# An attention layer followed by a graph aggregation on one core: bulk transfers moved from SP's queue to GpSimd's, and the places of eight maxima in VectorE's order changed

## What is computed

```python
q = x @ Wq.T + bq;  k = key @ Wk.T + bk;  v = value @ Wv.T + bv
s = (q @ k.T) / sqrt(4096) * adj
s = where(abs(s) < 1e-5, -1e9, s)
h = softmax(s, axis=-1) @ v @ Wm.T + bm
x1 = layernorm(x + h)
out = layernorm(x1 + relu((adj @ x1) @ W1.T + b1))
```

## Time and profile before

| | us |
|---|---|
| median of 3 executions | 2224.5 (2216.5 to 2249.4) |
| the profiled execution's own time | 2225.5 |
| its span in the trace | 2223.7 |
| TensorE matmul busy | 1986.5 (89%), 8859 matmuls |
| VectorE busy | 1545.2 (69%) |
| ScalarE busy | 872.4 (39%) |
| GpSimd busy | 107.2 (5%), 158 instructions |
| DMA queues | q1 (SP) 306.26 MB, 57.7% of the engines' span; q0 (GpSimd) 85.47 MB, 16.9% |

### The profile page before, as it was taken

One profiled execution on the slowest core, in us unless ns is written; L12 is line 12 of the kernel. 1 busy time (PEld: TensorE's weight loads), 2 busy tenths in 40 slices (PEclk: granted clock), 3 DMA queues, 4 the chain that ended last, 5 costly groups with the idle time before them and its releaser, 6 DMA issues.

```text
span 2223.7 us, 26354 instructions
## 1 busy us (share of the span) xinstructions
PE 1986.5 (89%) x8859; PEld 890.4 (40%) x8859; DVE 1545.2 (69%) x3203; ACT 872.4 (39%) x1166; POOL 107.2 (5%) x158
## 2 busy tenths in 40 slices
PE   8968998999999986989897878998897669999998
PEld 5423443444444432434333333443343224444443
DVE  7987777888888643767565656666665424888887
ACT  5765444556565433444443444444442210000000
POOL 5000000000000200000000000000000000000000
PEclk9998999999999997999999989999998889999999
DMA  8548877899999957678878798777777967555452
GB/s 304 192 143 195 227 212 197 202 260 247 260 246 257 254 129 192 126 154 159 153 145 143 144 142 154 154 164 155 141 152 153 228 168 206 119 134 144 118 124 75
DMA packets 585958, 393.21 MB, mean 177 GB/s; under 512 B 479728, under 2 KB 506352, under 8 KB 584048
## 3 DMA queue, kind: packets, MB, share of 16 engines
q1 hardware_dynamic: 565088, 306.26, 57.7%
q0 software_dynamic: 20752, 85.47, 16.9%
HBM read 190.32 MB, written 117.44 MB: 138 GB/s over the span
## 4 chain that ended last, share of the span: by engine, by line
PE 68%; DMA 10%; DVE 8%; SPq 7%; issue 5%; ACT 2%; DVEq 0%; ACTq 0%
PE ps L1042 21%; PE ps L1021 20%; PE ps L1181 15%; DMA UT<-Uhl 6%; PE ps L1053 5%; PE ps L1066 2%; PE ps L1136 2%; PE ps L974 1%; DMA PT<-Phl 1%; SPq L461 1%; SPq L457 1%; DMA x1T<-x1hl 1%; DVE prob L1937 1%; DMA kv_chunk<-in_key_t 1%; SPq L579 1%
## 5 line engine op out<-in xcount | busy, mean ns | idle before, releaser
L1042 PE MATMUL ps<-V,PT 128*128 128x512 f16 x3072 | 709.4, 381 | 7.2 <-issue 7.2
L1021 PE MATMUL ps<-KG,left 128*128 128x512 f16 x2688 | 639.8, 387 | 67.5 <-ACT ps L1378 50.9
L1042 PEld LDWEIGHTS ps<-V,PT 128*128 128x128 f16 x3072 | 301.9, 98 | 375.0 <-issue 16.7
L1021 PEld LDWEIGHTS ps<-KG,left 128*128 128x128 f16 x2688 | 266.6, 100 | 403.6 <-issue 89.9
L1385 ACT ACTIVATE small<-prob 128x512 f32<-128x512 f32 x256 | 159.1, 627 | 268.3 <-DVE prob L1937 247.7
L1965 DVE SCALAR_TENSOR_TENSOR Phl<-prob,Phl 128x2048 f16<-128x2048 f32 x64 | 146.6, 2290 | 119.6 <-ACT Phl L1398 111.9
L1053 PE MATMUL ps<-Wvm,UT 128*128 128x512 f16 x384 | 121.4, 482 | 120.9 <-issue 102.4
L1378 ACT ACTIVATE ps<-ps 128x512 f32<-128x512 f32 x192 | 111.5, 581 | 230.6 <-PE ps L1021 230.6
L1943 DVE TENSOR_SCALAR small<-small,eps_s,neg_s 128x512 f32<-128x512 f32 x256 | 137.1, 542 | 64.6 <-ACT small L1385 62.9
L2142 DVE SCALAR_TENSOR_TENSOR z_out<-ps,inv_vw,x_in 128x512 f32<-128x512 f32 x32 | 24.0, 751 | 225.8 <-PE ps L1053 225.8
L1398 ACT ACTIVATE Phl<-prob 128x2048 f16<-128x2048 f32 x64 | 121.8, 1904 | 143.7 <-DMA PT<-Phl 141.8
(11 more groups left out here) (222 smaller groups left out, 2005.6 us busy)
## 6 DMA issues: line engine op xcount, KB each, us to landing
adjh<-in_adj POOLq DMA_DIRECT2D x64, 512.0 KB, 8.1
adj_bf<-adjh SPq DMA_DIRECT2D x64, 512.0 KB, 6.0
left_dram<-left SPq DMA_DIRECT2D x16, 896.0 KB, 6.5
xraw<-in_x_t SPq DMA_DIRECT2D x8, 1024.0 KB, 8.7
t_dram<-tq POOLq DMA_DIRECT2D x8, 1024.0 KB, 5.5
t<-t_dram SPq DMA_DIRECT2D x32, 256.0 KB, 6.3
x_in<-in_x SPq DMA_DIRECT2D x32, 256.0 KB, 3.7
xb_dram<-x_in SPq DMA_DIRECT2D x32, 256.0 KB, 2.9
```

The lines of the kernel that those rows point to most:

```text
L1021: last = nc.tensor.matmul(ps[:, bank, :], left[:, s, k, d * P:(d + 1) * P], KG[gr][:, RIGHT[k], m, d, :], start=(first and n == 0), stop=( ...
L1042: last = nc.tensor.matmul(ps[:, BU + b, :], PT[:, b, s, m, :], V[:, v, m, :], start=(m == 0 and n == 0), stop=(m == MT - 1 and n == 2))
```

## The change

All plain loads and stores of both passes that stood in SP's list are issued on GpSimd's, by functions of the same names with the same waits and the same source and destination. SP keeps the transposes (and, in the aggregation, its loads of x1 rows and b1). The order of GpSimd's new list is written anew. VectorE's two maxima of a period change place, and a chunk is now loaded half a period earlier relative to its use. The load of W1 counts on another semaphore. SP's lists become:

```diff
                 for q in range(1, NP):
-                    first_period(q)
...
+                    for g in (2 * q - 2, 2 * q - 1):
+                        turn_high(g)
+                        turn_low(g)
...
                 def second_period(q):
                     i = q - NP
                     if i >= 2:
                         turn_merged_high(2 * i - 4)
                         turn_merged_low(2 * i - 4)
                     turn_high(2 * q - 2)
                     turn_low(2 * q - 2)
                     if i >= 2:
-                        load_o(2 * i - 2)
                         turn_x1_high(2 * i - 4)
-                        store_x1(2 * i - 4)
...
                         turn_x1_low(2 * i - 4)
                     turn_high(2 * q - 1)
                     turn_low(2 * q - 1)
                     if i >= 2:
                         turn_merged_high(2 * i - 3)
                         turn_merged_low(2 * i - 3)
...
                         turn_x1_high(2 * i - 3)
                         turn_x1_low(2 * i - 3)
-                    store_adj(q, 0)
-                    if q + 1 < 2 * NP:
-                        load_left(q + 1, True)
-                    store_adj(q, 1)
-                    if i >= 2:
-                        store_x1(2 * i - 3)
-                        store_y(2 * i - 4)
-                    if i >= 1:
-                        load_x_again(2 * i - 1)
```

GpSimd's new lists (in the first pass the list of SP before was `load_t`, the transposes of one block, xb, kp and left stores, adj stores, x load, the transposes of the other block, o store, xb store, chunk, x load, vp store, second loads, chunk, o store):

```diff
+                def first_period(q):
+                    load_adj(q, 0)
+                    store_left(q)
+                    if q + 1 < NP:
+                        load_t(q + 1)
+                    load_adj(q, 1)
...
+                    if q + 1 < NP:
+                        store_x_bias(2 * (q + 1))
+                    for b in range(2):
+                        store_adj(q, b)
+                    if q + 2 < NP:
+                        load_x_first(2 * (q + 2))
+                    if 2 <= q < 6:
+                        load_chunk(2 * (q - 2) + 1)
+                    if q == NP - 1:
+                        for k in range(NB):
+                            load_right(0, k)
+                    if q >= 2:
+                        store_first(2 * q - 3)
+                    if q + 1 < NP:
+                        store_x_bias(2 * (q + 1) + 1)
+                    if q + 2 < NP:
+                        load_x_first(2 * (q + 2) + 1)
+                    if FIRST_STEP <= q < FIRST_STEP + STEPS:
+                        store_second_keys(q - FIRST_STEP)
+                        store_second_values(q - FIRST_STEP)
+                    if 1 <= q < 5:
+                        load_chunk(2 * (q - 1))
+                    if q == FIRST_STEP - 1:
+                        pool.wait_ge(kv_mx, 4 * MC)
+                    if FIRST_STEP - 1 <= q < FIRST_STEP + STEPS - 1:
+                        load_second(q + 1 - FIRST_STEP)
+                    if q == NP - 1:
+                        pool.wait_ge(left_st, 16 * NP)
+                        for k in (P1, P7, P6, P2):
+                            load_right(1, k)
+                        load_left(NP, False)
+                        for k in (P5, P4):
+                            load_right(1, k)
+                        load_left(NP, True)
+                        load_right(1, P3)
+                    store_first(2 * q - 2)
...
+                def second_period(q):
+                    i = q - NP
                     for b in range(2):
                         load_adj(q, b)
...
+                    if i >= 3:
+                        store_y(2 * i - 5)
+                    if i >= 1:
+                        load_o(2 * i - 2)
                     for b in range(2):
+                        store_adj(q, b)
+                    if i >= 2:
+                        store_x1(2 * i - 4)
+                    if i >= 1:
+                        load_x_again(2 * i - 2)
+                    if i >= 3:
+                        store_sums(i - 3)
+                    if i >= 1:
+                        load_o(2 * i - 1)
+                    if q + 1 < 2 * NP:
+                        load_left(q + 1, False)
+                    if i >= 2:
+                        store_y(2 * i - 4)
+                    if i >= 1:
+                        load_x_again(2 * i - 1)
+                    if i >= 2:
+                        store_x1(2 * i - 3)
+                    if q + 1 < 2 * NP:
+                        load_left(q + 1, True)
```

At i = 0 the second list also loads W1 and stores a block of o; at i = 1 it loads V, chunks 0 to 2 together. In the last rows GpSimd's list mixes the remaining stores and loads with the seven `load_y`, and SP's adjacency parts go in twos:

```diff
-                for part in range(PARTS):
+                for part in range(2):
                     adj_part(0, 0, part)
-                store_y(NT - 5)
                 turn_x1_high(NT - 4)
-                store_x1(NT - 4)
                 turn_x1_low(NT - 4)
+                for part in range(2, PARTS):
+                    adj_part(0, 0, part)
```

VectorE in a period of the first pass:

```diff
                     prob_low(q - 1, 0)
+                    if 2 <= q < 6:
+                        second_maximum(2 * (q - 2))
...
+                    masked(q, 1, C11)
                     if 2 <= q < 6:
-                        second_maximum(2 * (q - 2))
-                    masked(q, 1, C11)
+                        second_maximum(2 * (q - 2) + 1)
...
-                    if 2 <= q < 6:
-                        second_maximum(2 * (q - 2) + 1)
```

More of the change, by code:

```diff
@@ L705, in _ @@
                 turn_x1_low(NT - 2)
-                store_x1(NT - 2)
                 sp.wait_ge(o_mm, 2 * NT - 1)
@@ new lines, in load_left, with load_x, load_x_first @@
+                def load_left(q, late):
+                    pool.wait_ge(s_sp, MADE * group(q - 1, 1) + (NB if late else P2 + 1))
+                    slots = slice(EARLY_LEFT, NB) if late else slice(0, EARLY_LEFT)
+                    pool.dma_start(left[:, :, slots, :], left_dram[q - NP, :, :, slots, :]).then_inc(left_in[late], 16)
+                def load_x(n, src):
+                    pool.dma_start(x_in[:, n % 2, :], src[n * P:(n + 1) * P, :]).then_inc(x_ld[n % 2], 16)
+                def load_x_first(n):
+                    wait(pool, xb_st[n % 2], 16 * (n // 2))
+                    load_x(n, x)
@@ new lines, in store_x_bias, with load_x_again, store_adj @@
+                def store_x_bias(n):
+                    pool.wait_ge(xb, n + 1)
+                    pool.dma_start(xb_dram[n * P:(n + 1) * P, :], x_in[:, n % 2, :]).then_inc(xb_st[n % 2], 16)
+                def load_x_again(n):
+                    wait(pool, s_z, n - 1)
+                    load_x(n, xb_dram)
+                def store_adj(q, b):
+                    n, half = 2 * (q % NP) + b, q // NP
+                    pool.wait_ge(adj_in[b], 16 * (q + 1))
+                    pool.dma_start(adj_bf[n * P:(n + 1) * P, half * HALF:(half + 1) * HALF], adjh[:, b, :]).then_inc(ab_st[b], 16)
@@ L843, in _, with first_start @@
                     load_adj(0, b)
+                for n in range(2):
+                    load_x_first(n)
                 store_t(7)
+                def first_start():
+                    for b in range(2):
+                        pool.wait_ge(t_st[b], 16 * (NG // 2))
+                    store_left(0)
+                    load_t(1)
+                    for n in range(2):
+                        store_x_bias(n)
+                    for n in range(2, 4):
+                        load_x_first(n)
+                    for b in range(2):
+                        store_adj(0, b)
@@ L845, in _ @@
+                first_start()
                 for q in range(1, NP):
+                    first_period(q)
+                def second_period(q):
+                    i = q - NP
                     for b in range(2):
                         load_adj(q, b)
[L849 to L854 removed]
@@ L868, in load_y @@
+                    if i >= 1:
[4 more added lines that the diff above has]
+                        load_left(q + 1, True)
+                    if i == 0:
+                        store_first(2 * q - 2)
+                for q in range(NP, 2 * NP):
+                    second_period(q)
                 def load_y(c):
@@ L883, in store @@
                     pool.dma_start(out[t * P:(t + 1) * P, :], y[:, k, :]).then_inc(out_st[k], 16)
-                for c in range(NT // TC - 1):
+                for c in range(3):
                     load_y(c)
+                load_o(NT - 2)
+                store_x1(NT - 4)
+                for c in range(3, 6):
+                    load_y(c)
+                store_y(NT - 5)
+                load_x_again(NT - 2)
+                load_o(NT - 1)
+                store_sums(NP - 3)
+                load_y(6)
+                store_x1(NT - 3)
+                load_x_again(NT - 1)
+                store_sums(NP - 2)
+                store_x1(NT - 2)
+                store_x1(NT - 1)
+                store_sums(NP - 1)
                 pool.wait_ge(ts_st, 16 * PT2)
```

255 lines of the change are left out of this document (75 added, 180 removed).

## The result

The changed kernel took 2268.06 us (median of 4 runs, 2255.87 to 2291.06) beside 2226.87 us of the kernel before on the same chip: a ratio of 1.017, interval 1.009 to 1.024. Another comparison gave 2272.28 beside 2228.94, ratio 1.022 (1.015 to 1.029). So it is about 2% slower, with both intervals above 1, where 2098 us was forecast; the range ended at 2190. The rows of after come from a profile of span 2265.0 us taken in the second comparison, since the first one fell into a disturbed run.

What follows compares the result with a forecast made beforehand. TensorE was taken to bound the kernel, with idle time waiting for transfers, mainly UT at `project`. 96 + 14 + 10 + 10 - 3 = 127 us off 2225.5 gave 2098 us, range 2062 to 2190.

Steps and rivals of the forecast that it cites:

- UT in the second pass: Transposes of merged rows, awaited by `project`, issue sooner on SP without bulk ahead: 96 us gained, bounds 0 and 110.
- Maxima: Periods 2 to 5: chunks loaded half a period ahead end VectorE's load waits: 14 us gained, bounds -4 and 21.
- Between the passes: First left blocks' load no longer stands behind two stores of o on SP: 10 us gained, bounds -10 and 25.
- after the second pass: From 1650 to 1860 us, SP loses bulk but keeps long adjacency transposes: 10 us gained, bounds -10 and 30.
- GpSimd's own time: 15 issues per second-pass period take 8.0 to 10.6 us on an idle engine; kp stores 1 us each, cost 0.
- Middle of the first pass: Nothing to win; t's load may come later behind adj and left on GpSimd: 9 periods x 0 to 2, cost 3 us.
- decides from 127/15: In the first pass, about 8 us of stall a period over 15 periods would cancel the 127 us gain.
- The slower rival: First pass: t's load behind adj and left on GpSimd comes 10 us late, +188 us, 2297 in all; chance 0.08.
- The 59 us: Second pass: by the skill's rule only SP's 4.9 us of issues ahead of UT are saved, over 12 periods.

Runs made afterwards that it cites:

- second_only: Changed kernel with the first pass's SP and GpSimd lists put back as before, maxima at their old place: 2110.22 us, ratio 0.947.
- best2: First pass's transfers on SP, second's on GpSimd, maxima moved, GpSimd waiting for a late PT pair before KG's second group of loads: 2097.85 us, ratio 0.944.
- t_first: Changed kernel with t's loads ahead of adj's first load and left's store on GpSimd in the first pass: 2354.16 us, ratio 1.056.
- first_only: Changed kernel with the second pass's SP and GpSimd lists put back as before: 2355.88 us, ratio 1.057.
- thin_left: Changed kernel with left's first-pass store cut from 896 to 128 KB from period 1 on (result not the reference's): 2252.12 us, ratio 1.010.
- sp_order: Changed kernel with SP's old first-pass order restored by GpSimd waits for both PT pairs, t and adj loads first: 2211.23 us, ratio 0.990.
- held_back: Changed kernel with t loaded first and the left and adj stores waiting for each first-pass period's first PT pair: 2216.59 us, ratio 1.003.

## Why the prediction was wrong, point by point

*UT in the second pass: right.* The forecast was 96 us; stage 18 to 30 lost 77.6 in the changed kernel, 67.0 in second_only and 90.1 in best2. UT lands in 3.6 us (median; before 6.4), and `project` waits 9.7 us in place of 101.8. A period is 52.6 us rather than the 50.4 forecast, at clock 0.99; 14.0 us of waits before `weigh` are new, perhaps the same sharing in small; that wasn't tried.

*Maxima: right in size* (14 forecast, 12 measured alone), though VectorE's wait for the chunks fell only from 15.5 to 9.8 us. *Between the passes* (10) measured 13.9, *after the second pass* (10) 17.7; both of these are one profile against another. *GpSimd's own time: right.* In the period above it issued at 0.54 to 0.86 us each; the kp store, taken at 1, took 1.11. (Of the 421 transfers counted, "8 x 32" are seven times 32; the total is right.)

*Middle of the first pass: the step that failed.* It read "Nothing to win, and thin cover" and took 3 us, "9 periods x 0 to 2". It measured 149 us in 15 periods, 9.9 us each; periods 5 to 13, nine of them, are 93 us longer. The step counted the load that changed its place (t) and left out the one that did not: PT. In SP's list the first pair of each period stood ahead of the period's stores, and what stood behind it in its own queue didn't delay it. There was a sign of it: in the earlier trace rows the DMA engines were 0.95 busy at 242 GB/s, and still the first pair's low halves landed in a median of 4.4 us, where a transpose alone takes 4.3 (a figure that only the later run gave). The text even had the mechanism, "leaving the queue gives no priority", with the 21.28 us of the earlier trace rows; but it applied this to UT, which left a queue full of bulk, and not to PT, for which the bulk left. With the slope measured here, 2.4 MB beside PT are 4.4 us, and with 2.5 of slow clock behind them 15 x 6.9 = 104 us if nothing covers them: most of the forecast gain. That counts one landing, and the pair has two in a row: it took 19.5 us in place of 8.2, 11.3 more. The rivals said it "decides from 127/15, about 8 us of stall a period"; it was 9.9.

*The slower rival* (2297) came nearest in time, with the wrong cause. It had t late by 10 us; t's wait is 32.8 us in 12 times over the whole span, and taking it away (t_first) made the kernel slower. That first_only is slower by 136 us is shown, and so is that the middle of the pass waits for the first pair of PT: in nine runs the period follows it. That the pair is late for bulk of another queue beside it rests on transfers alone, on thin_left, and on sp_order, where the delay moved to the second pair with the bulk. Two things are not separated: the burst in which GpSimd issues (2.4 MB in 3 us, just ahead of the pair) and the lost order. Open are the part of each landing that the bytes don't give, t_first's 82 us, and the early periods.

*The Trainium skill's rule* ("DMA: Bandwidth & Descriptors", section "Issuing engines are not separate DMA queues") says that transfers of all issuers interleave on the same engines and that spreading them only saves issue time. The first half agrees with the runs here (a transpose that lands in 4.3 us alone took 7.8 beside 2 MB of GpSimd's stores). The second half is what the measurement corrects: with the same bytes, spreading cost 136 us in one pass and gave 109 in the other, and by the runs above it also takes away an order and the pace at which SP issued. The 59 us that the prediction worked out from the rule for the second pass were exceeded too (67 to 90 measured).

## What to carry to other kernels

When bulk leaves a queue, look not only at the transfers that wait behind it but also at the small, urgent ones ahead of it: their place in the order can be their protection. A sign of it in this kernel was a transfer that landed near its time alone while the DMA engines were 0.95 busy. Look at each such transfer by its place in the period, since a median over all of them hid here which one was late. Here it paid to move bulk away from the queue where urgent transfers stood behind it (the second pass: -109 us) and to leave it where they stood ahead (the first pass: +136 us); decide stage by stage, and test each stage alone.

## What the runs showed of the hardware that I had not expected

A 512 KB transpose alone lands in 4.3 us, and each MB of bulk just issued on GpSimd's queue adds 1.8 us, up to 11.5 us with 4 MB, about the same for loads and stores; ahead of bulk in its own queue it stays at 4.3. SP issued eight stores of 512 KB in 7.89 us and eight loads in 3.72, GpSimd either in 4.2, and what 4 MB ahead cost went with this pace (6.7 us behind SP's stores, 11.4 to 12.9 in the other three). And in a full kernel what is held back by waits isn't free: it comes back as a burst, with PT's median at 15.0 us (held_back) where it was 8.6.
